# A two-layer transformer kernel on one core: constant rows copied from another queue, the context loads and squares moved a step later, and weights laid out later

## The reference, cut to what matters

```python
sa = _mha(x, x, swq, sbq, ..., mask, bias)          # self attention, band of 64 keys
x = _layernorm(x + sa, g1, be1)
ca = _mha(x, mem, cwq, cbq, ..., None, None)        # cross attention, 512 keys
x = _layernorm(x + ca, g2, be2)
ff = jax.nn.gelu(x @ w1 + b1, approximate=False) @ w2 + b2
x = _layernorm(x + ff, g3, be3)
# second layer
c_norm = context * rsqrt(mean(context * context) + EPS) * g_c
out = attention(rmsnorm(x, g_q) @ Wq, c_norm @ Wk, c_norm @ Wv) @ Wo
return rmsnorm(x + out, g_out)
```

## Time and profile before

| | us |
|---|---|
| median of 3 runs | 572.91 (572.53 to 574.24) |
| the profiled execution, its own time | 571.68 |
| its span in the trace | 569.9 |
| PE busy | 506.6 (89%) |
| DVE busy | 442.7 (78%) |
| ACT busy | 427.1 (75%) |
| POOL busy | 338.8 (59%) |

### The profile page before, as it was taken

How to read it: one execution, slowest core, us unless ns; L and a number is a source line. 1 busy time by engine, 2 the same in 40 slices (tenths; PEclk the granted TensorE clock), 3 DMA queues, 4 the chain that set the end, 5 groups by cost and what they waited for, 6 DMA issues and landing times.

```text
span 569.9 us, 17389 instructions
## 1 busy us (share of the span) xinstructions
PE 506.6 (89%) x6772; PEld 276.4 (49%) x6772; DVE 442.7 (78%) x911; ACT 427.1 (75%) x658; POOL 338.8 (59%) x640
## 2 busy tenths in 40 slices
PE   3577879877789999999999999999999999998984
PEld 2345556654434444455554545454545454444432
DVE  6335555646989999888889898989888999999912
ACT  3136666645367888989898989898898888787793
POOL 7344488883549627566576767675858384663032
PEclk9969999989989999999999999999999999999998
DMA  3957655564616347060615162425435361524000
GB/s 104 214 118 211 180 155 158 154 189 102 167 54 141 116 74 185 9 183 20 169 55 134 50 141 87 104 87 102 127 64 138 62 177 52 152 91 89 3 21 19
DMA packets 90195, 63.51 MB, mean 111 GB/s; under 512 B 6446, under 2 KB 89630, under 8 KB 90026
## 3 DMA queue, kind: packets, MB, share of 16 engines
q1 hardware_dynamic: 89540, 61.91, 42.0%
q10 hardware_dynamic: 574, 0.49, 0.5%
HBM read 34.99 MB, written 26.22 MB: 107 GB/s over the span
## 4 chain that ended last, share of the span: by engine, by line
PE 62%; DVE 8%; SPq 8%; ACT 7%; issue 6%; DMA 5%; POOL 4%; ACTq 0%; POOLq 0%; DVEq 0%
PE pv L646 20%; PE ps L627 11%; PE ps L582 10%; DVE negmax L945 6%; ACT probs L781 5%; PE ps L692 3%; PE ps L744 3%; PE ps L681 3%; PE ps L708 3%; DMA kst<-k_parts 2%; SPq L441 2%; PE ps L671 2%; PE ps L732 2%; SPq L466 2%; DMA qst<-mT 2%
## 5 line engine op out<-in xcount | busy, mean ns | idle before, releaser
L945 DVE TENSOR_REDUCE negmax<-ps 128x1 f32<-128x512 f32 x512 | 320.5, 683 | 25.7 <-PE ps L627 20.3
L781 ACT ACTIVATE probs<-ps 128x1024 f32<-128x1024 f32 x288 | 287.5, 1025 | 67.5 <-PE ps L582 40.5
L646 PE MATMUL pv<-probs,vp 128*32 128x256 f32 (+1 forms) x3072 | 158.6, 334 | 2.8 <-issue 2.8
L627 PE MATMUL ps<-kst,qst 61*128 61x512 bf16 x512 | 104.9, 385 | 8.5 <-DVE negmax L945 5.4
L582 PE MATMUL ps<-qst,kst 64*128 64x256 bf16 x1024 | 97.5, 273 | 6.5 <-ACT probs L781 3.1
L646 PEld LDWEIGHTS pv<-probs,vp 128*32 128x32 f32 x3072 | 70.4, 111 | 54.9 <-issue 28.1
L1056 POOL TENSOR_SCALAR mcap<-negmax 128x16 f32<-128x16 f32 x48 | 12.2, 254 | 107.4 <-DVE negmax L945 43.7
L582 PEld LDWEIGHTS ps<-qst,kst 64*128 64x128 bf16 x1024 | 38.7, 94 | 63.0 <-issue 21.8
L941 DVE TENSOR_REDUCE negmax<-ps 128x4 f32<-128x512 f32 x64 | 40.2, 684 | 27.5 <-PE ps L618 27.5
L627 PEld LDWEIGHTS ps<-kst,qst 61*128 61x128 bf16 x512 | 27.5, 93 | 58.9 <-DVE negmax L945 31.4
L1093 POOL TENSOR_TENSOR qr<-qf,qs 128x256 f32<-128x256 f32 x24 | 16.1, 670 | 58.2 <-ACT qs L805 31.3
(11 more groups left out here) (132 smaller groups left out, 762.8 us busy)
## 6 DMA issues: line engine op xcount, KB each, us to landing
kst<-k_parts SPq DMA_DIRECT2D x64, 192.0 KB, 4.3
qst<-q_parts SPq DMA_DIRECT2D x48, 192.0 KB, 3.8
k_parts<-ks SPq DMA_DIRECT2D x16, 384.0 KB, 2.7
q_parts<-qs SPq DMA_DIRECT2D x24, 192.0 KB, 2.2
cin<-in_ctx_dram SPq DMA_DIRECT2D x16, 256.0 KB, 3.0
k_parts<-ks SPq DMA_DIRECT2D x16, 256.0 KB, 3.1
q_parts<-qs SPq DMA_DIRECT2D x24, 128.0 KB, 2.3
k_parts<-ks SPq DMA_DIRECT2D x24, 128.0 KB, 3.2
```

The lines of the kernel that those rows point to most:

```text
L627: mm = nc.tensor.matmul(empty_banks("X", u.index, n + g), q[rows_in(g, 0, ROW_M), four, tile * P:(tile + 1) * P], k[rows_in(g, 0, ROW_M), ...
L646: mm = nc.tensor.matmul(pv[32 * j:32 * j + 32, dst:dst + n], vp[u.parity][:, c, 4 * quad + j, :], probs[:, quad, src:src + n], start=(quad ...
L781: nc.scalar.activation(to, src, ACT.Exp, scale=SCALE).then_inc(act_emptied, 1)
L945: ins = nc.vector.tensor_reduce(negmax[:, tile, at:at + 1], src, AX.X, ALU.max, negate=True)
```

## The change

Seven edits, all at the start and in the self stage but for two tokens.

1. The constant rows of stacks 1 and 2 are both copied from ACT's queue, ahead of ACT's copy of the first `V`. SP issues none, and waits for `stack_zeroed` in place of `stack_rows` before it loads a stack; PE still waits for `stack_rows`.
2. The loads of weights and constants (`win`, `cols`, `wo`, `rows`) go from SP's step 0, behind the second half of the maxima, to the end of its step -1, behind the first half of the maxima of unit 0.
3. The load of context rows for the squares goes from the early part of SP's step to its end, behind the stacks, and loads the batch of the current step, not of the next.
4. `C` in step i squares batch i-1, not batch i. Step 0 has none, and step 8 has one.
5. The weights of the other stages are laid out on DVE ahead of step 2, not before `B` in step 0.
6. In the first cross step a score tile goes behind a pair for the maxima.
7. In the last cross step one score tile takes banks 1 and 2, not 0 and 1.

```diff
-FIRST_SELF = ("XC:01 B3 raw V:1 ... S:12 M0:6 C X:53 P1 B:5 P2 O:0")
+FIRST_SELF = "XC:01 B3 raw V:1 ... S:12 M0:6 X:53 P1 B:5 P2 O:0"
-FIRST_CROSS: "... P0b X:04 S:12 X:36 V:5 A:2 S:01 X:36 X:54 ..."
+FIRST_CROSS: "... P0b C X:04 S:12 X:36 V:5 A:2 X:36 S:01 X:54 ..."
-LAST_CROSS = ("S:45 S:01 B3 ..."
+LAST_CROSS = ("S:45 S:12 B3 ..."
...
             elif name == "C":
-                yield "context", self.main, None, at
+                yield "context", self.before if 0 < self.i <= B else None, None, at
...
                 if n.index < STACKS:
-                    sp.wait_ge(stack_rows[n.stack], STACK_ROWS[n.stack])
+                    sp.wait_ge(stack_zeroed[n.stack], 2)
...
-                if s.i == 0:
-                    sp.dma_start(win[:, 3:9, :], a["w_in"][:, 3:9, :]).then_inc(win_rest, 16)
-                    sp.dma_start(cols[:, :], a["columns"]).then_inc(cols_loaded, 16)
-                    for dst, src in const_loads():
-                        sp.dma_start(dst, src).then_inc(consts_loaded, 16)
...
-                if s.main is not None and s.main.stage == 0:
-                    for batch in (0, 1) if s.i == 0 else (s.i + 1,):
-                        if batch < B:
-                            load_early(batch)
...
-                if s.i == -1:
-                    sp.wait_ge(ones_loaded, 64)
-                    sp.wait_ge(stack_zeroed[1], 2)
-                    copy_rows(sp, 1)
...
                 if s.nxt is not None:
                     load_maxima(s.nxt, 0)
+                if s.i == -1:
+                    sp.dma_start(cols[:, :], a["columns"]).then_inc(cols_loaded, 16)
+                    for dst, src in const_loads():
+                        sp.dma_start(dst, src).then_inc(consts_loaded, 16)
+                    sp.dma_start(win[:, 3:9, :], a["w_in"][:, 3:9, :]).then_inc(win_rest, 16)
                 if s.n is not None and not early:
                     load_stacks(s.n)
+                if s.main is not None and s.main.stage == 0:
+                    load_early(s.main.batch)
...
+            def copy_constant_rows():
+                act.wait_ge(ones_loaded, 64)
+                act.wait_ge(stack_rows[0], STACK_ROWS[0])
+                for i in range(1, STACKS):
+                    act.wait_ge(stack_zeroed[i], 2)
+                    copy_rows(act, i)
...
-                if s.i == 0:
-                    act.wait_ge(ones_loaded, 64)
-                    act.wait_ge(stack_rows[0], STACK_ROWS[0])
-                    act.wait_ge(stack_zeroed[2], 2)
-                    copy_rows(act, 2)
...
+                        if what == "V" and u.index == 0:
+                            copy_constant_rows()
                         take(what, u)
...
             for s in STEPS:
                 if s.i == 2:
+                    other_weights()
                     make_key_mask()
...
                         if what == "B":
-                            other_weights()
+                            bias_columns()
```

More of the change, by code:

```diff
@@ L73 @@
 SECOND_STEP = "XC:23 Q:0 K:2 X:45 X:64 V:0 M0:5 X:64 X:56"
-FIRST_SELF = ("XC:01 B3 raw V:1 Q:4 S:01 M1:5 X:32 K:1 S:12 X:30 X:26 D:5 A:5 S:45 P0 S:12 M0:6 C X:53 P1 B:5 P2 "
-              "O:0")
+FIRST_SELF = "XC:01 B3 raw V:1 Q:4 S:01 M1:5 X:32 K:1 S:12 X:30 X:26 D:5 A:5 S:45 P0 S:12 M0:6 X:53 P1 B:5 P2 O:0"
 SELF = "C B3 XC:56 V:0 raw Q:3 S:45 M1:1 D:0 K:1 X:43 S:56 X:21 P0 X:04 S:23 P1 A:5 M0:0 S:34 X:51 O:2 P2"
@@ L86 @@
 FIRST_CROSS = ("S:01 XC:34 B3 X:24 raw S:01 Q:5 X:36 X:16 S:23 M1:1 X:46 X:01 S:23 P0a sq X:64 X:05 S:23 T:5 K:1 D:6 "
-               "S:23 X:45 S:01 P0b X:04 S:12 X:36 V:5 A:2 S:01 X:36 X:54 P1a S:23 X:10 S:56 P1b X:12 S:34 P2a S:56 "
+               "S:23 X:45 S:01 P0b C X:04 S:12 X:36 V:5 A:2 X:36 S:01 X:54 P1a S:23 X:10 S:56 P1b X:12 S:34 P2a S:56 "
                "M0:2 X:34 O:0 S:12 P2b S:45 X:61 S:23 P3a")
-LAST_CROSS = ("S:45 S:01 B3 raw S:45 M1:2 S:23 S:45 P0a S:01 S:56 D:2 S:01 P0b S:56 S:34 S:01 S:56 P1 A:0 S:34 S:12 "
+LAST_CROSS = ("S:45 S:12 B3 raw S:45 M1:2 S:23 S:45 P0a S:01 S:56 D:2 S:01 P0b S:56 S:34 S:01 S:56 P1 A:0 S:34 S:12 "
               "S:56 P2 S:23 O:4 P3a")
@@ L916, in other_weights, with bias_columns @@
                 weights_of(1)
-                dve.wait_ge(cols_loaded, 16)
                 weights_of(2)
                 nc.vector.tensor_scalar(w["v2"], win[:, 8, :], cols[:, 5:6], None, ALU.mult).then_inc(v_weights, 1)
+            def bias_columns():
+                dve.wait_ge(cols_loaded, 16)
                 dve.wait_ge(zero_set, 1)
```

## The result

The changed kernel took 611.03 us (median of 4, 605.29 to 612.17) against 572.72 us before: 1.0651 times as long, 95% interval 1.0589 to 1.0713. The profiled execution is the one of 605.29 us, the shortest of the four; the other three took 610.67 to 612.17. Its span is 603.5, which is 33.6 us more than the 569.9 of before. Times in this document are medians over all executions of a kernel, while ratios and their intervals leave out the few executions in a slower state, more than 1.5% above the kernel's fastest.

The account below looks back on a forecast made before the run. The self stage was taken as bound by a near round trip through ACT, GpSimd and SP; the new loop's 32.0 us, 0.4 and 0.1 on 571.68 gave 604.2, plus 1.2 for the median: 605.4 us, range 593 to 617.

Parts of the forecast that it names:

- The loop: Steps 1 to 5: load last on SP and squares first on ACT wait for each other, 20.4 us a round.
- From the squares to the maxima: Part of each round, from ACT's squares to SP's issue of the maxima: 10.5 us, plus 1.9 for the clock.
- the clock's 1.9: Added to each round because PE's matmul clock halves while idle: 1.9 us, for two projections plus one score tile.
- The rival with the clock held: Clock holds or returns at once in steps 1 to 5: 1.9 us less a round, 597.8 us, chance 22%.
- the one with the whole round slow: Rival: slow clock costs 4 us instead of 1.9 in each of four rounds, 613.8 us, chance 13%.
- The pauses: Pauses in PE's issue in steps 1 to 5: 1.2 us added in two of the four rounds.
- Maxima to load, and landing: Rest of each round: 4.5 us from SP's maxima to the load's issue, 3.5 us for its 256 KB to land.
- Loss of the four rounds: Step 1 to step 5: 84.0 us against 52.04 before, a loss of 32.0 us.
- The start: Step 0: earlier stack loads gain 3.0 us at PE's first score tile, eaten at the first border; net +0.1.
- The landing at the first border: Load for the squares between steps 0 and 1: lands 3.5 us after issue, at 48.0 to 50.9 with the squares.
- Steps 7 and 8: Later load in step 7 costs 0 to 1 us, four squares in step 8 0 to 1.7; together 0.4.
- The cross stages: From step 8 on: as long as before, within 1 us.

Follow-up runs that it names:

- e5: The changed kernel run again, unaltered, for a second profile: 606.52 us, ratio 1.0600.
- e2: The kernel before with only the load moved to the end of SP's step and the squares a step later: 611.32 us, ratio 1.0691.
- e3: The changed kernel with the load for the squares at the head of SP's step, squares still first on ACT: 566.62 us, ratio 0.9916.
- e6: The changed kernel with the squares behind K in steps 1 to 5, load still last on SP: 571.2 us, ratio 0.9985.
- e4: The changed kernel with 24 extra matmuls ahead of Q in steps 1 to 5, keeping PE busy: 599.9 us, ratio 1.0487.
- e7: e3 with SP copying stack 1's constant rows again and ACT those of stack 2 in step 0: 569.75 us, ratio 0.9956.
- e1: The changed kernel with the squares and the load of their context rows put back as before: 567.85 us, ratio 0.9927.
- e11: e3 with the squares behind K in steps 1 to 5, so load first and squares later: 566.98 us, ratio 0.9932.
- e10: e3 with the other stages' weights laid out before the bias columns in step 0 again: 568.67 us, ratio 0.9954.
- e9: e3 with the two token changes in the cross steps undone: 567.99 us, ratio 0.9944.

## Why the prediction was right, and where it was off

The forecast was 605.4 us, in a range of 593 to 617. The median is 611.03, 5.6 us above the forecast and inside the range, and the mechanism is the one forecast. The profiled execution was put at 604.2 and took 605.29, but this closeness is partly luck, since the errors of the steps cancel:

| stretch | forecast | measured | difference |
|---|---|---|---|
| start to step 1 | +0.1 | +1.95 | +1.9 |
| step 1 to 5 | +32.0 | +28.27 | -3.7 |
| step 5 to 6 | 0 | +0.07 | +0.1 |
| step 6 to 8 | +0.4 | +2.25 | +1.9 |
| step 8 to the end | 0 | +1.06 | +1.1 |

The median was put 1.2 us above the profiled execution and lies 5.7 above it. No trace covers that difference; e5's profile, of another short execution, doesn't have it either. By the steps of the prediction:

- **The loop.** Shown by e2, e3 and e6. Of the signs named ahead, ACT's idle time in steps 1 to 5 is there (6.6 to 8.5 us, forecast 5 to 7, so a little longer), the copies of `xc` are 19.8 to 20.5 us apart (forecast 20.5), and the clock is at 0.50 after each idle time.
- **From the squares to the maxima.** Forecast 10.5 + 1.9 us. In the profile it is 12.57, 11.42, 11.96 and 12.24, mean 12.05, so the forecast is 0.35 too much. e4, with the clock held, has 10.31 for the stretch, so 10.5 was right for the part without the clock, and the clock's 1.9 is near the upper end of the 1.0 to 2.0 us that e4 shows for it. The rival with the clock held is out, and so is the one with the whole round slow (4 us).
- **The pauses.** 1.2 us more were put down for two of the four rounds. The trace has such a round once: the one with a pause of 1.47 us in PE's issue is 1.15 longer than the next, the other pair differs by 0.3. And the mean of 12.05 above holds the pauses already, so the whole 2.4 us are too much. With four times 0.35 they make 3.8 us, about all of the 3.7 by which the rounds were too dear.
- **Maxima to load, and landing.** 4.68 us in the mean against 4.5, and 3.35 against 3.5.
- **Loss of the four rounds.** Forecast 32.0, measured 28.27, and 30.6 in the second profile (e5).
- **The start.** This step failed in its working, though its sum was off by only 1.9 us. The first score tile was to come near 30.3 us. It came at 32.91. PE's timelines, before and after, show why:

```profile
18.40 0.64 PE L609 MATMUL ps<-band,identb 64*64 64x512 bf16 x4 [7.37 <-DMA kst<-k_parts]
```

```profile
19.58 0.64 PE L602 MATMUL ps<-band,identb 64*64 64x512 bf16 x4 [8.56 <-DMA kst<-k_parts]
...
32.91 0.39 PE L557 MATMUL ps<-identb,band 64*128 64x512 bf16 x2 [1.01 <-DMA qst<-mT]
...
34.66 0.70 PE L674 MATMUL ps<-xc,w0k 128*128 128x256 f32 x2 [0.33 <-ACT probs L774]
```

And SP's timeline after:

```profile
17.37 3.79 SPq L432 DMA_DIRECT2D q_parts<-qs  x3
...
41.14 1.48 SPq L484 DMA_DIRECT2D qst<-mT  x2
```

ACT issues its copies from 14.93 us on, in the middle of the first stacks, and SP's three stores of q then take 3.79 us to issue, where they took 2.00 at this place before. `kst` landed about 1.2 us later than before, and PE's whole program with it. The other traces bear this out. From the start of SP's first store to PE's first tile on `kst` it is 8.3 to 8.5 us in the three kernels in which SP copies the rows of stack 1 (before, e2, e7), and 9.0 to 10.1 in the ten in which ACT copies rows early. The gain at the first tile was 0.4 us, not 3.0. ACT's idle time ahead of its first copy of V, which was to be no longer than before, grew from 7.72 to 8.90 us. The rule cited from the Trainium skill, DMA: Bandwidth & Descriptors, "Issuing engines are not separate DMA queues" (another queue saves issue time, not transfer time), was the one to count with. This trace agrees, with `kst` 1.2 us late while the copies are under way.

What made up for it is the clock. Before, PE ran step 0 at the slow level from 33 to past 42 us. After, it ran at the fast one: the projection K takes 0.70 us in place of 1.22. So the maxima of unit 1 went out at 41.14. With a fast clock the prediction's bound for them was 38.3, and 2.6 us for the late first tile make it 40.9. The clock goes with the wait for the maxima in most traces. In the five in which PE waited 2.0 to 4.0 us for them (before, e1, e2, e7, e11) it has slow matmuls behind that wait, though in e2 the clock had fallen ahead of it. In seven of the eight with a wait of at most 1.4 us PE is fast from 35 us on. The eighth is e10, which is slow to past 43 us after a wait of 0.82, so a short wait does not ensure the fast clock.
- **The landing at the first border.** 4.3 us, from 45.61 to 49.92, against 3.5.
- **Steps 7 and 8.** Forecast 0.4. Step 6 to 7 took 2.73 more. The squares of step 7 waited 2.42 us, since the load came behind stacks of the cross stage and landed 5.7 us after its issue at 160.64, where 3.5 was assumed for all. Of the terms that were put too low it has the largest error, and it hides in the total because the four rounds were 3.7 us too dear.
- **The cross stages.** From step 8 on they were to stay as long as before within 1 us. They took 1.06 more, just outside, and nothing here says why.
- **Weights and tiles.** Put at 0. In the changed kernel ACT's wait for the load covers them. With the loop open the weights show as 0.86 us in PE's wait (e10); the tiles are not resolved (e9).

## What to carry to other kernels

A transfer that only a side job needs becomes the bound of the kernel when it is last in one in-order list and its user is first in another: follow the list of the issuing queue to its end, and compare that time with the moment at which the other engine reaches the user. Either end opens the loop, and moving the load (e3) did better than moving its user (e6): some 40 us against the changed kernel, to 35. Price a stall with what it does to the matmul clock as well, here 1 to 2 us a round.

## What the runs showed of the hardware

- Useless matmuls in a wait made the kernel faster, by 6 to 9 us of some 610: 24 matmuls, of which the trace has 23 in 5.13 us, kept the granted clock at 1.00 over a border that otherwise ended at 0.50.
- The level of the clock in step 0 can differ between executions of kernels that are alike up to there: K took 0.70 us in e3 and 1.22 in e10, and step 1 began 5.8 us later in e10. The column of the granted clock read 1.00 in e10 all that time; its first fall is shown between 47 and 48 us. So ahead of the first change in a trace the durations of equal matmuls have to be read beside that column.
- Row copies from ACT's queue, eight issues in 6 us, lengthened the issue of SP's three stores to 3.79 us from the 2.00 at the same place before. In the ten traces with such copies, four or eight of them, the three stores took 3.0 to 4.3 us, in the three without 1.8 to 2.0.
